# An attention and sparse-FFN layer on one core: wk_t and the token rounding on ScalarE, a product of norms on VectorE, a result buffer per group, four fillers, new orders

## The reference, cut to what matters

```python
h = _layernorm(x, axis=-1) * (1 + ca) + sa
x = x + ga * attn(h)          # q, k, v, causal softmax, ctx @ Wo + bo
h = _layernorm(x, axis=-1) * (1 + cb) + sb
x = x + gb * ffn(h)           # relu(h @ w1.T + b1), 4 of 16 blocks kept, @ w2 + b2
```

## Time and profile before

| | us |
|---|---|
| median of 3 runs (113.32 to 114.53) | 113.36 |
| the profiled execution | 113.37 |
| its span, first to last instruction | 111.6 |
| TensorE busy | 107.3 (96%) |
| GpSimd busy | 89.4 (80%) |
| VectorE busy | 85.8 (77%) |
| ScalarE busy | 75.5 (68%) |

### The profile page before, as it was taken

The page is one execution under the profiler, slowest core; times in us unless marked ns, Lnnn a source line. Parts: engine busy times, 40 slices in busy tenths (PEclk is TensorE's granted clock), DMA queues, the critical chain, the costliest instruction groups (busy, mean ns, idle before and its releaser), DMA issues.

```text
span 111.6 us, 2065 instructions
## 1 busy us (share of the span) xinstructions
PE 107.3 (96%) x609; PEld 89.4 (80%) x609; DVE 85.8 (77%) x318; ACT 75.5 (68%) x166; POOL 89.4 (80%) x122
## 2 busy tenths in 40 slices
PE   6979999999999999999999999999999999999991
PEld 6968677898888878888688787887978888887790
DVE  6789999979999898999789923981599772871651
ACT  1636499589882588759499786899954468646710
POOL 5366899989999989989997999999999659947000
DMA  2996000000000000000000000000000000000444
GB/s 53 257 323 170 0 3 6 0 0 0 3 9 0 0 0 0 0 0 3 0 0 6 0 0 0 0 0 0 0 6 0 3 3 0 0 0 6 132 126 117
DMA packets 6021, 3.42 MB, mean 31 GB/s; under 512 B 886, under 2 KB 5625, under 8 KB 6010
## 3 DMA queue, kind: packets, MB, share of 16 engines
q1 hardware_dynamic: 5434, 3.03, 9.4%
q10 hardware_dynamic: 576, 0.26, 0.8%
HBM read 2.24 MB, written 1.05 MB: 29 GB/s over the span
## 4 chain that ended last, share of the span: by engine, by line
PE 76%; POOL 15%; DMA 2%; DVE 2%; issue 2%; ACT 1%
PE bank L945 12%; PE bank L941 12%; PE bank L942 12%; POOL p_lo L522 11%; PE bank L1056 5%; PE bank L1043 5%; PE bank L1044 5%; PE bank L1005 5%; DMA x<-in_L_attn_y_all_dram 2%; PE bank L1088 2%; PE bank L968 2%; POOL rstd L432 2%; PE bank L1154 2%; PE bank L1183 1%; POOL rstd L442 1%
## 5 line engine op out<-in xcount | busy, mean ns | idle before, releaser
L522 POOL TENSOR_TENSOR p_lo<-p_full,p_hi 128x512 fp32r<-128x512 f32 (+2 forms) x36 | 42.8, 1213 | 1.1 <-ACT p_full L643 1.1
L643 ACT ACTIVATE p_full<-bank 128x512 f32<-128x512 f32 (+2 forms) x36 | 20.5, 568 | 3.8 <-POOL p_lo L522 3.8
L636 ACT ACTIVATE p_hi<-bank 128x512 fp32r<-128x512 f32 (+2 forms) x36 | 20.5, 570 | 3.5 <-PE bank L1056 2.1
L528 POOL TENSOR_TENSOR hid_lo<-hid_full,hid_hi 128x512 fp32r<-128x512 f32 x12 | 15.3, 1284 | 2.6 <-ACT hid_hi L672 2.6
L765 DVE TENSOR_REDUCE cmax<-bank 128x1 f32<-128x512 f32 x24 | 16.2, 684 | 0.8 <-PE bank L1005 0.6
L1043 PE MATMUL bank<-g_hi,zt_hi 128*128 128x512 f32 (+3 forms) x40 | 15.0, 376 | 0.0
L1056 PE MATMUL bank<-g_lo,zt_hi 128*128 128x512 f32 (+3 forms) x40 | 14.6, 369 | 0.0
L1044 PE MATMUL bank<-g_hi,zt_lo 128*128 128x512 f32 (+3 forms) x40 | 14.6, 364 | 0.0
L945 PE MATMUL bank<-p_lo,z_hi 128*128 128x512 f32 (+2 forms) x36 | 13.8, 384 | 0.2 <-POOL p_lo L522 0.2
L1005 PE MATMUL bank<-zt_hi,g_hi 128*128 128x512 f32 (+3 forms) x40 | 13.9, 381 | 0.0
L941 PE MATMUL bank<-p_hi,z_hi 128*128 128x512 f32 (+2 forms) x36 | 13.9, 385 | 0.0
(11 more groups left out here) (219 smaller groups left out, 258.2 us busy)
## 6 DMA issues: line engine op xcount, KB each, us to landing
x<-in_L_attn_y_all_dram SPq DMA_DIRECT2D x3, 256.0 KB, 3.4
out_dram<-res SPq DMA_DIRECT2D x3, 256.0 KB, 2.3
w<-in_L_ffn_w_dram SPq DMA_DIRECT2D x2, 256.0 KB, 4.3
x<-in_L_attn_y_all_dram SPq DMA_DIRECT2D x2, 128.0 KB, 2.9
wmod<-in_L_wmod_dram SPq DMA_DIRECT2D x1, 256.0 KB, 3.8
...
```

Of the source, the lines that this page charges most:

```text
L522: pool.tensor_tensor(p_lo[:, s, w:], p_full[:, n % 2, w:], p_hi[:, s, w:].bitcast(F32), ALU.subtract).then_inc(p_lo_pool, 1)
L528: pool.tensor_tensor(hid_lo[:, m, :], hid_full[:, n % 2, :], hid_hi[:, m, :].bitcast(F32), ALU.subtract).then_inc(hid_lo_pool, 1)
L636: nc.scalar.activation(p_hi[:, s, w:], src, ACT.Exp).then_inc(p_hi_s, 1)
L643: nc.scalar.activation(p_full[:, n % 2, w:], src, ACT.Exp).then_inc(p_full_s, 1)
```

## The change

ScalarE's `z1` now copies `wk_t` too, behind `wq_t`; VectorE's `z2` is gone. GpSimd's `u` no longer rounds the tokens: ScalarE has a new word `u` (`token_high`) that writes `z_hi`, and GpSimd's `u` waits for it and subtracts. For norms 4 to 7 GpSimd makes only the power; VectorE has a new word `e` (`shift_mean`), one instruction that multiplies mean by -1 and by rstd, and ScalarE's `a4` to `a7` wait for that. `res` has a buffer for each group, and the waits on earlier stores are gone. TensorE has fillers `i10` to `i13`. All four lists are in a new order; of these the lines that matter below are shown.

```diff
 TENSOR_PLAN = """
-i0 z0 z10 z1 i1 i2 i3 i4 f0 z2 i5 f1 i6 i7 i8 i9 z6 q0 z4 z3 a0 a1 a2 a3 p0 n1 z7 b0 q1 p1 s0 p2 a4 a5 s1 z5
-a6 s2 a7 s3 w0 a8 a9 n2 w1 a10 w2 a11 w3 p4 p6 z9 b1 q2 z8 o0 s4 n3 a12 p5 a13 s5 s6 a14 s7 a15 a16 s8 w4 a17
...
-h9 d6 n7 d7 h10 r3 h11 d8 d9 y0 m3 h12 h13 y1 v12 v13 d10 d11 h14 v14 h15 v15 d12 y2 d13 d14 d15 t0 y3 t1
+i0 z0 i1 z10 i2 z1 i3 i4 i10 i11 f0 i12 i13 z2 f1 i5 i6 i7 i8 i9 z6 q0 z4 z3 a0 a1 a2 a3 n1 p0 z7 b0 q1 p1 s0
+p2 a4 s1 a5 z5 s2 a6 s3 a7 w0 a8 n2 a9 w1 w2 a10 w3 a11 p6 p4 p5 b1 z9 q2 o0 s4 z8 a12 n3 a13 s5 s6 a14 s7 a15
...
+d4 y0 m2 h8 h9 d5 d6 n7 h10 d7 r3 d8 d9 h11 y1 m3 h12 h13 v12 v13 d10 d11 h14 v14 h15 v15 d12 d13 y2 d14 d15
+t0 y3 t1
...
 SCALAR_PLAN = """
-z0 z2 z1 j0 z3 j1 z6 q0 z4 z11 n1 a2 q1 e0 z5 z9 e1 z13 e2 e3 n2 c0 z12 a3 q2 z8 e4 e5 e6 n3 e7 e8 q3 e9 e10
-e11 c1 e12 e13 e14 e15 e16 e17 e18 e19 a4 e20 e21 n4 e22 e23 z7 a5 e24 c2 e25 e26 m0 e27 e28 n5 e29 h0 e30 e31
...
+z0 z2 z1 j0 z3 j1 q0 u0 z4 z6 z11 n1 a2 z9 q1 e0 z5 e1 u1 e2 u2 z13 e3 c0 n2 z12 a3 q2 e4 z8 e5 n3 e6 e7 q3 e8
+e9 e10 e11 e12 e13 c1 e14 u3 e15 e16 a4 e17 e18 e19 z7 e20 n4 e21 e22 a5 e23 e24 e25 c2 e26 e27 m0 n5 e28 a6
...
 VECTOR_PLAN = """
-j0 j1 z1 a0 a1 z2 g1 u0 z3 u1 g2 v1 z10 s0 s1 s2 s3 q0 n1 b0 g3 s4 s5 z5 s6 s7 q1 s8 s9 s10 s11 n2 b1 x0 s12
-s13 s14 q2 s15 s16 n3 s17 i8 s18 s19 i9 s20 s21 i10 s22 s23 s24 i11 b2 s25 s26 z6 s27 s28 s29 g4 s30 s31 x1 q3
-s32 s33 g5 s34 i20 i21 s35 s36 s37 i22 s38 n4 s39 i23 b3 m0 c0 x2 g6 h0 n5 m1 h1 c1 h2 i36 h3 i37 n6 i38 h4 m2
-i39 c2 h5 x3 g7 h6 h7 h8 h9 n7 h10 m3 c3 h11 k12 f0 k13 f1 k14 k15 f2 t0 f3 t1
+j0 j1 z1 a0 a1 g1 u0 z3 u1 g2 v1 s0 z10 s1 s2 s3 q0 n1 b0 g3 s4 s5 z5 s6 s7 q1 s8 s9 s10 s11 n2 b1 x0 s12 s13
+s14 q2 s15 s16 n3 s17 s18 i8 s19 s20 i9 s21 i10 s22 s23 s24 b2 i11 s25 z6 s26 s27 s28 s29 g4 x1 e4 s30 g5 s31
+s32 q3 s33 s34 i20 s35 s36 s37 i21 n4 s38 s39 i22 e5 b3 i23 m0 c0 x2 g6 h0 n5 e6 m1 h1 c1 h2 i36 i37 n6 i38
+i39 h3 m2 c2 h4 h5 x3 g7 h6 h7 e7 h8 h9 n7 h10 m3 c3 h11 f0 f1 k12 k13 k14 k15 f2 f3 t0 t1
...
 GPSIMD_PLAN = """
-z0 z7 j0 j1 z1 p1 p2 z6 u0 l0 z8 l1 l2 p3 z13 z4 u1 l4 l5 l6 l7 z11 l8 l9 l10 z10 u2 l12 l13 l14 l15 l16 l17
-p4 l18 l19 p5 l20 l21 l22 u3 l24 l25 l26 z9 l27 p6 l28 l29 l30 l31 k0 l32 l33 k1 l34 k2 l35 l36 l37 l38 k3 k4
...
+z0 z1 j0 j1 z7 p1 p2 z8 u0 z6 l0 l1 l2 p3 z13 z11 u1 l4 l5 u2 l6 l7 l8 l9 l10 z4 l12 l13 l14 p4 l15 l16 l17
+l18 l19 p5 l20 l21 l22 z9 u3 l24 l25 l26 l27 p6 z10 l28 l29 l30 l31 l32 l33 k0 l34 k1 l35 l36 l37 l38 k2 k3 k4
...
...
         y_sb = sb("y_sb", [P, 2, GW])
-        res = sb("res", [P, 2, GW])
+        res = sb("res", [P, NG, GW])
         future, unseen = sb("future", [P, GW]), sb("unseen", [P, P])
 
...
         dve_step, pool_step = sem("dve_step"), sem("pool_step")
-        xt_mm, nt_hi_s, nt_lo_s, z_tok_s = sem("xt_mm"), sem("nt_hi_s"), sem("nt_lo_s"), sem("z_tok_s")
+        xt_mm, nt_hi_s, nt_lo_s, z_hi_s, z_tok_s, shifted_mean = (
+            sem(n) for n in ("xt_mm", "nt_hi_s", "nt_lo_s", "z_hi_s", "z_tok_s", "shifted_mean"))
         q_mm, q_hi_s, q_lo_s = sem("q_mm"), sem("q_hi_s"), sem("q_lo_s")
 
...
             queue.dma_start(out_tiles[NG - 1][:, t:t + 1, :],
-                            res[:, (NG - 1) % 2, t * P:(t + 1) * P].rearrange("p (i d) -> p i d", d=D)).then_inc(stored[NG - 1], 16)
+                            res[:, NG - 1, t * P:(t + 1) * P].rearrange("p (i d) -> p i d", d=D)).then_inc(stored[NG - 1], 16)
 
         block = ctx.enter_context(nc.Block())
...
                 sp.dma_start(out_tiles[g][:, part.start // P:part.stop // P, :],
-                             res[:, g % 2, part].rearrange("p (i d) -> p i d", d=D)).then_inc(stored[g], 16)
+                             res[:, g, part].rearrange("p (i d) -> p i d", d=D)).then_inc(stored[g], 16)
             store_row(sp, 1)
             for g in range(NG):
...
                 pool.wait_ge(stats, n + 1)
-                if scalar_applies(n):
+                if scalar_applies(n) and n < NG:
                     ahead(pool.tensor_scalar(neg_mean[:, k, t], mv[:, k, t, 0], -1.0, None, ALU.mult))
                 step(pool.tensor_scalar(rstd[:, k, t], mv[:, k, t, 1], EPS, None, ALU.add))
                 last = pool.tensor_tensor(rstd[:, k, t], rstd[:, k, t], pow_half[:], ALU.pow)
-                if scalar_applies(n):
+                if scalar_applies(n) and n < NG:
                     step(last)
                     last = pool.tensor_tensor(mean_rstd[:, k, t], neg_mean[:, k, t], rstd[:, k, t], ALU.mult)
...
             def token_halves(g):
-                pool.wait_ge(*norm_applied(g))
-                step(pool.tensor_copy(tokens(z_hi, g), norm_rows(g)))
+                pool.wait_ge(z_hi_s, g + 1)
                 pool.tensor_tensor(tokens(z_lo, g), norm_rows(g), tokens(z_hi, g).bitcast(F32),
                                    ALU.subtract).then_inc(z_tok_s, 1)
...
                     nc.scalar.copy(wq_t[:], score_bank[1][:, 0:P]).then_inc(wqk_t_s, 1)
+                    act.wait_ge(wqk_mm, 2)
+                    nc.scalar.copy(wk_t[:], score_bank[2][:, 0:P]).then_inc(wqk_t_s, 1)
                 elif i == 3:
                     act.wait_ge(fold_mm, 1)
...
                 k = n // NG
-                act.wait_ge(power_s, n + 1)
+                if n < NG:
+                    act.wait_ge(power_s, n + 1)
+                else:
+                    act.wait_ge(shifted_mean, n - NG + 1)
                 if n == 0 or n == NG:
                     act.wait_ge(ones_made, n // NG + 1)
...
                 nc.scalar.copy(grp(g_hi, g), proj_bank[:]).then_inc(q_hi_s, 1)
+
+            def token_high(g):
+                act.wait_ge(*norm_applied(g))
+                nc.scalar.copy(tokens(z_hi, g), norm_rows(g)).then_inc(z_hi_s, 1)
 
             def exps(t):
...
 
-            run(SCALAR_PLAN, {"z": prepare, "j": first_high, "a": apply, "n": norm_high, "q": q_high, "e": exps, "c": ctx_copy,
+            run(SCALAR_PLAN, {"z": prepare, "j": first_high, "a": apply, "n": norm_high, "q": q_high, "u": token_high, "e": exps, "c": ctx_copy,
                               "m": keep_copy, "h": hidden, "y": y_copy})
 
...
                 last.then_inc(xn_by_dve, 1)
+
+            def shift_mean(n):
+                k, g = n // NG, n % NG
+                t = slice(g * GT, g * GT + GT)
+                dve.wait_ge(power_s, n + 1)
+                nc.vector.scalar_tensor_tensor(out=mean_rstd[:, k, t], in0=mv[:, k, t, 0], scalar=-1.0, in1=rstd[:, k, t],
+                                               op0=ALU.mult, op1=ALU.mult).then_inc(shifted_mean, 1)
 
             def first_low(i):
...
                 g, part = n, result_part(n)
-                if g >= 2:
-                    dve.wait_ge(stored[g - 2], 16)
                 dve.wait_ge(y_turned, n + 1)
-                nc.vector.tensor_tensor(res[:, g % 2, part], result_bank(n)[:, part],
+                nc.vector.tensor_tensor(res[:, g, part], result_bank(n)[:, part],
                                         tokens(x, g).rearrange("p i d -> p (i d)")[:, part], ALU.add).then_inc(res_s, 1)
 
...
                                                    in1=base[:, 1:], op0=ALU.mult, op1=ALU.add).then_inc(lift_s, 1)
-                elif i == 2:
-                    dve.wait_ge(wqk_mm, 2)
-                    nc.vector.tensor_copy(wk_t[:], score_bank[2][:, 0:P]).then_inc(wqk_t_s, 1)
                 elif i == 3:
                     dve.wait_ge(fold_hi_s, 1)
...
                     dve.wait_ge(x_due_s, 1)
-                    dve.wait_ge(stored[NG - 3], 16)
                 dve.wait_ge(row_mm, i + 1)
-                nc.vector.tensor_tensor(res[:, (NG - 1) % 2, t * P:(t + 1) * P], row_bank(i)[:, 0:P], x_due[:, i, :],
+                nc.vector.tensor_tensor(res[:, NG - 1, t * P:(t + 1) * P], row_bank(i)[:, 0:P], x_due[:, i, :],
                                         ALU.add).then_inc(row_res_s, 1)
 
...
             nc.vector.memset(nmax[:, 1:, 0:P], 0.0).then_inc(ones_made, 1)
-            run(VECTOR_PLAN, {"z": prepare, "j": first_stat, "a": first_apply, "v": apply, "u": first_low, "g": norm_stats, "n": norm_low, "q": q_low, "s": row_max, "b": shift,
+            run(VECTOR_PLAN, {"z": prepare, "j": first_stat, "a": first_apply, "v": apply, "u": first_low, "g": norm_stats, "e": shift_mean, "n": norm_low, "q": q_low, "s": row_max, "b": shift,
                               "i": hide, "l": split, "x": attention_out, "m": logits, "c": choose, "h": hidden, "k": hidden_low, "f": finish, "t": row_finish})
 
```

More of the change, by code:

```diff
@@ L43 @@
 TENSOR_PLAN = """
-i0 z0 z10 z1 i1 i2 i3 i4 f0 z2 i5 f1 i6 i7 i8 i9 z6 q0 z4 z3 a0 a1 a2 a3 p0 n1 z7 b0 q1 p1 s0 p2 a4 a5 s1 z5
-a6 s2 a7 s3 w0 a8 a9 n2 w1 a10 w2 a11 w3 p4 p6 z9 b1 q2 z8 o0 s4 n3 a12 p5 a13 s5 s6 a14 s7 a15 a16 s8 w4 a17
-s9 a18 w5 a19 q3 a20 s10 a21 w6 a22 s11 a23 w7 a24 w8 b2 w9 a25 w10 w11 s12 a26 s13 s14 a27 a28 s15 a29 w12
-s16 a30 a31 s17 w13 o1 s18 w14 a32 s19 a33 w15 s20 a34 a35 s21 w16 a36 w17 a37 s22 n4 a38 s23 a39 w18 w19 w20
```

(28 more changed lines are left out.)

## The result

The changed kernel took 114.98 us (median of 4 runs, 114.14 to 115.37) against 113.38 before: a ratio of 1.011, with an interval of 1.006 to 1.016. The forecast was 112.7, the range 111.9 to 113.8, so the change is slower where a small gain was forecast. The profiled execution of after (114.14) and that of before (113.37) are both of the quick group, so in this pair the change costs 0.77 us. The last product of TensorE starts at 109.72 us where it started at 108.98: 0.74 of the 0.77 lies on TensorE.

What follows compares the result with a forecast made beforehand. The prediction took TensorE, busy 96% of the span, as the bound; 113.37 - 0.20 (start) - 0.30 (c) - 0.10 (result buffers, d) - 0.10 (new orders, b) = 112.67, say 112.7 us, range 111.9 to 113.8.

Steps and rivals of the forecast that it cites:

- The start: Before q0: wk_t on ScalarE and four fillers bring the fold 0.5 to 0.6 us earlier, of which 0.20 arrives.
- case A: Rival: everything closes, the fold's 0.5 us arrives and three other TensorE gaps go; 111.8 to 112.3 us, chance 0.18.
- (c): TensorE's third pass at 55.45 instead of 55.11 us, waiting for GpSimd's low half: 0.34 at most, 0.3 taken as gain.
- ScalarE's casts at 0: Token rounding moved from GpSimd to ScalarE, four casts, 2.5 us in all: cost taken as 0, bounds 0 to 0.8.
- (b): A row-maximum product on TensorE waits for VectorE to free a bank: at most 0.3 us, 0.1 taken from new orders.
- (d): At the end, VectorE's result additions stand ahead of a low half that frees TensorE's bank: gain 0 to 0.2, 0.1 taken.
- The four e words at 0: Mean times rstd for norms 4 to 7 on VectorE: 0.1 us taken, hidden by 1.36 free between 44 and 55.5 us.
- case C: Rival: VectorE held at e4 and e5 by GpSimd's splits or late power; 114.9 us (114 to 115), chance 0.12.
- e4: VectorE's mean times rstd for norm 4, among row maxima: GpSimd's power expected done by its turn; hold 0 to 1.3 us.
- e5: VectorE's mean times rstd for norm 5, in order ahead of row maxima it can hold up; hold 0 to 1.3 us.
- e6: VectorE's mean times rstd for norm 6, in order ahead of hidden products it can hold up; hold 0 to 1.3 us.

Runs made afterwards that it cites:

- the one-input version: Changed kernel with VectorE's mean times rstd as four one-column instructions, rstd as a per-partition scalar: 113.18 us, ratio 0.997 to the kernel before (earlier run 114.25, 0.999).

## Why the prediction was wrong, point by point

- **The start** was right in mechanism and size: the third pass of q0 is 0.26 earlier for 0.20, and with the start alone 0.2 arrive. VectorE, not the fold, is late next, as it said. But when VectorE's chain is shortened by 0.5, TensorE's turning of w1 leaves 0.16 of it: the 0.5 of case A was out of reach for a second reason.
- **(c)**, 0.30: right. The wait at 55.45 is gone (0.41 of standstill before, none after), and the run with the norms back on GpSimd brought it back.
- **ScalarE's casts at 0**: right as a cost. What was missing is their worth: the prediction counted GpSimd's relief only at 55 us, but with the casts back on GpSimd the same orders lose 1.2 us, first at the gate near 16 us.
- **(b) and (d)**, 0.10 each: not found. A wait for a row maximum of 0.3 stays in the one-input version. The additions f0 and f1 do stand at 100.95 now, but from 101 to 105 us TensorE stands still 0.57 us, 0.53 before. The gain of (d) is not there; no run changes the buffers alone.
- **The four e words at 0** is the step that failed. The term was "0.1, which the free 1.36 us hide"; the rows say 1.25, 0.73 and 1.12, together 3.1 us, on an engine that had 1.36 free around the first two. TensorE's busy time in 13 to 55 us fell from 41.96 to 41.68 us, which the prediction had named as a sign of being wrong. This is case C, which had a chance of 0.12. It named the place, the mechanism and the point from which it decides (0.7 us per instruction); it also bounded the price by one split of 1.3, which is what was measured. Two things stood against it. One was "the power is done before e4's turn": it ended at 44.80, e4 began at 44.83, and the split behind the power was ahead of it. The other was "four columns are little to hold", and that sentence is the error. The width of the held instruction has no part in the price: what is waited for is the rest of GpSimd's instruction, 1.29 us long for 512 columns and never far from the next. The row at 39 us of the earlier trace rows does not say so either; it was misread as "both engines were longer". First GpSimd's split there by itself, then the same instruction of VectorE in the changed kernel with GpSimd's splits after it:

```profile
39.43 1.90 POOL L522 TENSOR_TENSOR p_lo<-p_full,p_hi 128x512 fp32r<-128x512 f32 x1 [0.51 <-ACT p_full L643]
```

```profile
38.18 1.07 DVE L915 TENSOR_TENSOR w_full<-w_full,b_row 1x512 f32<-1x512 f32 x1
...
39.17 2.54 POOL L523 TENSOR_TENSOR p_lo<-p_full,p_hi 128x512 fp32r<-128x512 f32 x2 [1.38 <-ACT p_full L653]
```

VectorE's 1.06 us are that instruction's own length: it takes 1.07 in the changed kernel too, where the split begins only 0.08 before its end. In the kernel before only the split was longer, 1.90 us in place of 1.29, and it was the one that began second, with 0.74 us of VectorE's left. So the row showed one engine waiting for the other, not two that share. Nor was the rule of the Trainium skill that the prediction cited there ("SBUF — State Buffer", "Who interferes with whom") given its weight: it calls the sharing an exclusive lock. The rows beside the splits agree.

- Even so case C put the price at 114.9 where 114.14 was profiled against 113.37. It let the whole hold of e4 and e5 beyond the free time arrive, 1.7 us. What arrived is 0.69, all of it at e4, and 0.45 for e6, whose hold case C did not count.

With the hold out, the sum nearly stands: the one-input version was profiled at 112.79, and the sum without any hold was 112.67. That is in part luck: the start and (c) gave 0.26 and 0.41 at their places where 0.20 and 0.30 were taken, and (b) and (d) nothing where 0.20 was. As a median it is 113.18 against 113.47 on the same chip, a ratio whose interval just reaches 1; in the quick group it is 0.4 us below before. It is the best version found. Not settled is the 0.15 us by which the changed kernel is behind it already at o0, in both pairs of profiles, although no word up to there differs: in the quick pair it comes in between 13.8 and 14.8 us, in the later pair near 9.5.
